# Two score matmuls per batch in place of three, with Q's halves stacked on the partitions

## The reference, cut to what matters

```python
x = x + einsum('bct,bcd->bdt', x, L0_weights[conditions])        # x is (32, 128, 1024)
q, k, v = (proj(x, W) for W in (Wq, Wk, Wv))                      # 16 heads of 64
q = q * minimum(cond, 4.0)                                        # one factor per batch
scores = einsum('bhqd,bhkd->bhqk', q, k) / sqrt(64)
scores = where(causal, scores, finfo.min)
attn = softmax(scores, axis=-1)
x = x + einsum('bsd,ed->bse', (attn @ v), Wo)
```

## Time and profile before

| | before |
|---|---|
| median of 3 runs | 1558.01 us (1557.51 to 1558.75) |
| the profiled execution | 1558.96 us |
| its span | 1557.5 us |
| TensorE busy | 1547.1 us, 99% |
| VectorE busy | 1034.9 us, 66% |
| ScalarE busy | 840.9 us, 54% |
| GpSimd busy | 866.6 us, 56% |
| granted TensorE clock, mean | 0.998 of 2.4 GHz |

### The profile page before, as it was taken

The page is one execution under the profiler, slowest core; times in us unless marked ns, Lnnn a source line. Parts: engine busy times, 40 slices in busy tenths (PEclk is TensorE's granted clock), DMA queues, the critical chain, the costliest instruction groups (busy, mean ns, idle before and its releaser), DMA issues.

```text
span 1557.5 us, 23477 instructions
## 1 busy us (share of the span) xinstructions
PE 1547.1 (99%) x7459; PEld 1302.0 (84%) x7459; DVE 1034.9 (66%) x1891; ACT 840.9 (54%) x2286; POOL 866.6 (56%) x752
## 2 busy tenths in 40 slices
PE   9999999999999999999999999999999989999999
PEld 7888888888888888888888888888888878888887
DVE  5867677664477777777767777777777644555553
ACT  6666566652466666666655666666666622222220
POOL 1555665662365566557655576575577545555552
PEclk9999999999999999999999999999999999999999
DMA  9968988866766677767677466677665696444442
GB/s 324 335 230 278 319 307 296 294 254 231 273 190 198 201 214 209 205 184 191 182 240 229 147 179 202 194 200 200 180 188 157 237 366 226 162 168 163 162 167 83
DMA packets 192300, 341.46 MB, mean 219 GB/s; under 512 B 23986, under 2 KB 116402, under 8 KB 185010
## 3 DMA queue, kind: packets, MB, share of 16 engines
q1 hardware_dynamic: 191026, 331.59, 66.2%
q10 hardware_dynamic: 1152, 8.39, 1.4%
HBM read 184.70 MB, written 134.22 MB: 205 GB/s over the span
## 4 chain that ended last, share of the span: by engine, by line
PE 95%; DVE 2%; DMA 1%; SPq 1%; POOL 0%; issue 0%; ACT 0%; DVEq 0%; POOLq 0%
PE p_PJ L768 22%; PE p_PJ L769 22%; PE p_PJ L770 22%; PE p_SC L770 6%; PE p_SC L769 6%; PE p_SC L768 6%; PE p_PV L873 4%; PE p_LP L768 1%; PE p_PV L768 1%; PE p_PV L770 1%; PE p_PV L769 1%; PE p_LP L770 1%; PE p_LP L769 1%; DVE t_WSL L1285 1%; DVE t_TS L1281 1%; DMA out<-t_xr 0%
## 5 line engine op out<-in xcount | busy, mean ns | idle before, releaser
L769 PE MATMUL p_PJ<-t_XL,t_WH 128*128 128x512 f32 x1008 | 394.2, 391 | 0.0
L768 PE MATMUL p_PJ<-t_XH,t_WH 128*128 128x512 f32 x1008 | 394.2, 391 | 0.0
L770 PE MATMUL p_PJ<-t_XH,t_WL 128*128 128x512 f32 x1008 | 392.1, 389 | 0.0
L1118 ACT ACTIVATE t_PP<-t_PP,t_st 128x128 f32<-128x128 f32 x512 | 199.5, 391 | 174.9 <-DVE t_st L1314 173.3
L1438 POOL TENSOR_TENSOR t_PP<-t_PP,t_st 128x512 f32<-128x512 f32 x128 | 133.2, 1041 | 205.8 <-DVE t_st L1318 205.8
L770 PEld LDWEIGHTS p_PJ<-t_XH,t_WL 128*128 128x128 f32 x1008 | 189.3, 188 | 40.5
L768 PEld LDWEIGHTS p_PJ<-t_XH,t_WH 128*128 128x128 f32 x1008 | 190.0, 188 | 33.8
L769 PEld LDWEIGHTS p_PJ<-t_XL,t_WH 128*128 128x128 f32 x1008 | 190.0, 188 | 32.3
L1332 DVE TENSOR_REDUCE t_AT<-p_PV 64x256 f32<-64x512 f32 x252 | 171.3, 680 | 24.5 <-ACT t_AC L1136 12.1
L1444 POOL TENSOR_TENSOR t_AT<-t_AT,t_AC 128x256 f32<-128x256 f32 x126 | 117.1, 929 | 126.2 <-DVE t_AT L1332 126.2
L1441 POOL TENSOR_TENSOR t_PS<-t_PT,t_PS 128x512 fp32r<-128x512 f32 x122 | 157.6, 1292 | 0.0
(11 more groups left out here) (259 smaller groups left out, 3597.7 us busy)
## 6 DMA issues: line engine op xcount, KB each, us to landing
t_XH<-xth_scratch SPq DMA_DIRECT2D x56, 512.0 KB, 6.4
t_XL<-xtl_scratch SPq DMA_DIRECT2D x56, 512.0 KB, 6.7
t_PT<-t_TB SPq DMA_DIRECT2D x580, 32.0 KB, 2.3
v_scratch<-t_VR SPq DMA_DIRECT2D x64, 256.0 KB, 4.6
xth_scratch<-t_XH SPq DMA_DIRECT2D x16, 1024.0 KB, 4.5
xtl_scratch<-t_XL SPq DMA_DIRECT2D x16, 1024.0 KB, 6.8
t_VX<-v_scratch SPq DMA_DIRECT2D x32, 512.0 KB, 5.6
at_scratch<-t_AT SPq DMA_DIRECT2D x126, 128.0 KB, 3.4
```

What stands on the lines that cost most here:

```text
L768: pe.matmul(bank, lh, rh, start=first, stop=False, skip_group_check=goes_on)
L769: pe.matmul(bank, lh, rl, start=False, stop=False, skip_group_check=goes_on)
L770: return pe.matmul(bank, ll, rh, start=False, stop=last, skip_group_check=goes_on)
L1118: act.activation(PP[:, u, h, :], PP[:, u, h, :], ACT.Exp, bias=st[:, 0, u, h:h + 1], scale=1.0, accum_out=st[:, 1, u, h:h + 1]).then_inc(a ...
```

## The change

The two operands are stacked in another way. For each head h there is one tile `QM[h]` whose 64 rows of that head hold Q's high part, and whose other 64 rows hold Q's low part of the same head. `KM[h]` has 256 columns for each batch: the first 128 hold K's high part in all 128 rows (twice, once for each half of the rows), the last 128 hold K's low part in the head's rows and zero in the others. One matmul of 256 columns for each head then gives high by high plus low by high in its first 128 columns, and high by low in its last 128. The two are added by VectorE: first the low product with the mask into `PP`, then the high product, in place, waiting on the first. The scores of the batches go round three banks (SC0, SC1 and LP), one for each batch, where two batches shared a bank.

The due times change with it: Q is evicted later, `a` is 7 steps after the end of the K block in place of 5, and scores, masks and exps are spread out. The K evictions stay at 0.25 and 1 step after the block. `QM` and `KM` stand for `QH`, `QL`, `KH`, `KL`, with the same sizes.

```diff
-                late = 2.5 if n else 0
+                late = 5 if n else 0
                 q_ev.put(done + late, n)
                 ql_ev.put(done + late + 1, n)
                 done += 8
                 kh_ev.put(done + 0.25, n)
                 kl_ev.put(done + 1, n)
-                a = done + 5
+                a = done + 7
                 for u in range(GB):
-                    k = u // 2
-                    sc_at.put(a + k, GB * n + u)
-                    mask_at.put(a + 1 + 2 * k, GB * n + u)
-                    exp_at.put(a + (2, 3, 4, 5)[u], GB * n + u)
-                move_at.put(a + 10, n)
+                    sc_at.put(a + (0, 0.5, 1, 3.5)[u], GB * n + u)
+                    mask_at.put(a + (1, 2, 3, 4.75)[u], GB * n + u)
+                    exp_at.put(a + (2.25, 3.25, 4.25, 6)[u], GB * n + u)
+                move_at.put(a + 10.25, n)
                 for k in range(2):
                     P = 2 * n + k
-                    recip_at.put(a + 4 + 2 * k, P)
-                    norm_at.put(a + 4.25 + 2 * k, P)
-                    turn_at.put(a + 7.5 + 1.5 * k, P)
+                    recip_at.put(a + (5, 7)[k], P)
+                    norm_at.put(a + (5.25, 7.25)[k], P)
+                    turn_at.put(a + (8, 9.75)[k], P)
                     last = n == 4 * NGRP - 1
-                    half_at.put(a + (20 if last else 25.25) + 0.5 * k, P)
-                    ptl_at.put(a + (20.75 if last else 26) + 1.5 * k, P)
-                    v = a + (27.25 + 3.25 * k if last else 29 + 4.5 * k)
+                    half_at.put(a + (22.5 if last else 25.25) + 0.5 * k, P)
+                    ptl_at.put(a + (23.25 if last else 26) + 1.5 * k, P)
+                    v = a + (29.25 + 3.25 * k if last else 29 + 4.5 * k)
                     own = v + (1.75 if n >= 4 * NGRP - 2 else (1.75, 8.5)[k])
...
-            early = t - PAIR
+            early = t - PAIR + (5 if q == 0 else 0)
...
+            if U == 2:
+                pe.wait_ge(dve_X, 2 * B)
+            if U >= 3:
+                pe.wait_ge(dve_s, U - 2)
+            for h in range(2):
+                mm = pe.matmul(s_bank(U)[:, h].rearrange("p l k -> p (l k)"), QM[h][:, cols], KM[h][:, u, :], start=True, stop=True)
+            mm.then_inc(pe_sc, 1)
...
-                        act.activation(KH[r, :, 128 * h:128 * h + 128], pj[r], ACT.Copy).then_inc(act_k, 1)
+                        other = slice(64 - 64 * h, 128 - 64 * h)
+                        act.activation(KM[h][r, :, 0:128], pj[r], ACT.Copy).then_inc(act_k, 1)
+                        act.activation(KM[h][other, :, 0:128], pj[r], ACT.Copy).then_inc(act_k, 1)
...
-                    act.activation(QH[:], PJ[bank_of["q", n]][:], ACT.Copy).then_inc(act_q, 1)
+                    for h in range(2):
+                        r = slice(64 * h, 64 * h + 64)
+                        act.activation(QM[h][r], PJ[bank_of["q", n]][r, :], ACT.Copy).then_inc(act_q, 1)
...
-                        dve.wait_ge(act_k, 2 * n + h + 1)
-                        dve.tensor_tensor(KL[r, :, k], pj[r], KH[r, :, k].bitcast(f32), ALU.subtract).then_inc(dve_k, 1)
+                        dve.wait_ge(act_k, 4 * n + 2 * h + 2)
+                        dve.tensor_tensor(KM[h][r, :, 128:256], pj[r], KM[h][r, :, 0:128].bitcast(f32), ALU.subtract).then_inc(dve_k, 1)
                 for n in ql_ev(tick):
-                    dve.wait_ge(act_q, n + 1)
-                    dve.tensor_tensor(QL[:], PJ[bank_of["q", n]][:], QH[:].bitcast(f32), ALU.subtract).then_inc(dve_q, 1)
+                    for h in range(2):
+                        r, other = slice(64 * h, 64 * h + 64), slice(64 - 64 * h, 128 - 64 * h)
+                        dve.wait_ge(act_q, 2 * n + h + 1)
+                        dve.tensor_tensor(QM[h][other], PJ[bank_of["q", n]][r, :], QM[h][r].bitcast(f32), ALU.subtract).then_inc(dve_q, 1)
...
+                    dve.scalar_tensor_tensor(out=PP[:, u], in0=s_bank(U)[:, :, 1], scalar=beta[:, bb:bb + 1],
+                                             in1=mask[:].unsqueeze(1).to_broadcast([128, 2, 128]), op0=ALU.mult, op1=ALU.add).then_inc(dve_l, 1)
+                    dve.wait_ge(dve_l, U + 1)
+                    dve.scalar_tensor_tensor(out=PP[:, u], in0=s_bank(U)[:, :, 0], scalar=beta[:, bb:bb + 1],
+                                             in1=PP[:, u], op0=ALU.mult, op1=ALU.add).then_inc(dve_s, 1)
```

More of the change, by code:

```diff
@@ L162, in cond_attention @@
             LATE = tile
[L163 to L166, removed]
+        KM = [sb(f"KM{h}", [128, GB, 256], f32r) for h in range(2)]
+        QM = [sb(f"QM{h}", [128, T], f32r) for h in range(2)]
         with nc.sbuf_tensor("t_PS", [128, 8, 2, 128], f32r) as tile:
@@ L205, in cond_attention @@
         act_Y, pool_Y = sem("y_high"), sem("y_low")
+        dve_l = sem("s_low_masked")
         dve_s, dve_m, act_e, dve_r = sem("masked"), sem("row_max"), sem("exp"), sem("row_recip")
@@ L654, in operand @@
             else:
-                halves = QH[:], QL[:]
+                halves = QM[0][:], QM[1][:]
             return tuple(four(h) for h in halves)
@@ L758, in pe_wait_bank @@
             if kind == "q":
-                pe.wait_ge(dve_q, i + 1)
+                pe.wait_ge(dve_q, 2 * i + 2)
             elif kind == "k":
@@ L848, in pe_v_step, with s_bank @@
                 mm.then_inc(pe_P, 1)
+        def s_bank(U):
+            return (SC[0], SC[1], LP)[U % 3][:].rearrange("p (h l k) -> p h l k", h=2, l=2)
         def pe_scores(U):
@@ L854, in pe_scores @@
                 pe.wait_ge(dve_k, 2 * n + 2)
+                pe.wait_ge(act_k, 4 * n + 4)
             if U == 0:
@@ L1181, in dve_turn @@
                 dve.wait_ge(s_O, 32 * 32)
+                dve.wait_ge(l_P, 160 * n)
             elif k == 0:
@@ L1301, in dve_program @@
                     bb = GROUP[n // NC] * GB + u
+                    dve.wait_ge(pe_sc, U + 1)
+                    if U == 0:
+                        dve.wait_ge(l_const, 32)
+                        dve.wait_ge(dve_beta, 1)
                     if n and u == 0:
                         dve.wait_ge(dve_t, 2 * n)
-                    dve.wait_ge(pe_sc, GB * n + 2 * (u // 2) + 2)
-                    if U == 0:
-                        dve.wait_ge(l_mask, 16)
-                        dve.wait_ge(dve_beta, 1)
-                    dve.scalar_tensor_tensor(
-                        out=PP[:, u], in0=SC[u // 2][:, 256 * (u % 2):256 * (u % 2) + 256].rearrange("p (h k) -> p h k", h=2), scalar=beta[:, bb:bb + 1],
-                        in1=mask[:].unsqueeze(1).to_broadcast([128, 2, 128]), op0=ALU.mult, op1=ALU.add).then_inc(dve_s, 1)
+                    dve.scalar_tensor_tensor(out=PP[:, u], in0=s_bank(U)[:, :, 1], scalar=beta[:, bb:bb + 1],
[3 more added lines that the diff above has]
+                                             in1=PP[:, u], op0=ALU.mult, op1=ALU.add).then_inc(dve_s, 1)
                 for U in mask_at(tick):
@@ L1404, in pool_program @@
                         pool.wait_ge(s_x1[z], 16 * x1_stores(z))
[L1405 to L1406 removed]
+                    pool.memset(KM[0][:].bitcast(f32), 0.0).then_inc(pool_z, 1)
+                    pool.memset(KM[1][:].bitcast(f32), 0.0).then_inc(pool_z, 1)
                 if tick == (T_ATT - 8) * TICK:
@@ L1730, in sp_program @@
                 if tick == 0:
-                    sp.dma_start(mask[:], mask_d).then_inc(l_mask, 16)
-                    sp.dma_start(beta[:], cond.to_broadcast([128, B])).then_inc(l_cond, 16)
+                    sp.dma_start(mask[:], mask_d).then_inc(l_const, 16)
+                    sp.dma_start(beta[:], cond.to_broadcast([128, B])).then_inc(l_const, 16)
                 for bb in l0_load(tick):
```

10 lines of the change are left out of this document (3 added, 7 removed).

## The result

| | before | after |
|---|---|---|
| median | 1558.38 us (4 runs, 1557.51 to 1559.41) | 1788.9 us (4 runs, 1785.96 to 1789.71) |
| ratio | | 1.148 (95% interval 1.146 to 1.150) |
| span of the profiled execution | 1557.5 us | 1786.9 us |
| mean granted clock | 0.998 | 0.941 |

The change costs 230 us. The forecast was 1664 and the range ended at 1710: the direction was right, the size was not. The page of the changed kernel: busy time of the engines, and the chain that ended last.

The account below looks back on a forecast made before the run. TensorE bounds the kernel before; afterwards VectorE's chain through own1 makes it wait. 48 x 1.80 + 13 x 1.60 = 107.2, less 1.4, gives +105.8: 1664 us against the median, range 1612 to 1710.

Parts of the forecast that it names:

- The two ties: Own1 queues behind K's low part on VectorE, half of P behind a K eviction on ScalarE; even PV awaits both.
- Who releases the PV: Own1, VectorE's reduction into AT, releases the even PV in 61 cells; TensorE idles 2.05 us a cell.
- the sum: Loop from even PV to next: 14.93 us against 13.33, +1.60 a cell, +1.80 in cells with a split.
- 1.3 us idle in the first 5 us left the clock at 1.00, and 2 us lies nearer to that: Argument against TensorE's clock falling when it idles 2.05 us in each attention cell.
- case B: TensorE's clock falls after the idle: 1817 us if in every cell, 1703 in a quarter; chance 0.12.
- a mild B: Clock falling in only some cells, which the range takes in; a quarter of the cells gives 1703 us.
- The price of the unknown operation: VectorE's second scale-and-add, four a cell: taken at 0.473 to 0.477 us; ends 0.41 (1649) and 0.69 (1717).
- The rule weighed: Skill page's rule that VectorE semaphores cost nothing extra: would save 0.9 us, loop 14.05; forecast kept 0.11 a hand-off.
- Rival A: VectorE hand-offs are cheap and the boundary after a K block paces the cell: 14.31 us, 1616 in all; chance 0.17.
- Rival C: TensorE stays the bound, own1 and half of P done within 12.88 us: faster, 1528 us; chance 0.03.
- bare VectorE work already 0.3 over: VectorE's work of 13.2 us a cell, without waits, exceeds the 12.86 TensorE would need.
- Rival D: No change: the saved 0.47 us a cell and the stall cancel; chance 0.02.

Follow-up runs that it names:

- the version of 1553.8: Changed kernel reordered (masks in pairs, splits earlier), then second half of P later and GpSimd's norm and low half ahead of its A^T product: 1553.8 us, ratio 0.997.
- the run with nine filler matmuls: Changed kernel plus nine unread 512-column matmuls on TensorE ahead of each even PV's wait: 1700.7 us, clock 0.998.

## Why the prediction was wrong, and where it was right

- **The two ties**: right. Each is enough for a slow loop (1673.2 in the kernel before with own1's alone, 1721.2 with the half of P's alone), and undoing both takes 174 us off.
- **Who releases the PV**: right. Own1, 62 times; idle 2.15 us where 2.05 was forecast, and 2.58 with a split where the sum has 2.25. The half of P comes under it, by 0.6 to 0.7 us and not by the forecast's 0.5 and 0.2: at full clock its chain gives cells of 14.56 and 15.10, own1's 15.27 and 15.67.
- **The step that failed: "1.3 us idle in the first 5 us left the clock at 1.00, and 2 us lies nearer to that".** The clock fell in all cells of the loop but one, which is case B, given 0.12. The cost was 88 us. B was over-priced for every cell (153) and under-weighted as a case; the range reached only "a mild B". This is why 1789 lay outside it. Full clock would have given about 1701, inside.
- **Its evidence was misread too.** The clock column of the earlier trace rows says 1.00, but the nine matmuls of that stretch took 647 ns on average:

```profile
L948 PE MATMUL p_PJ<-t_PRH 128*128 128x512 f32 x9 | 4.2, 647 | 1.3 <-POOL t_PRH L1397 1.3
```

The same shape takes 0.63 us at 1.2 GHz (905.31 in the rows of after) and 0.39 at 2.4 GHz, so TensorE ran that stretch slowly whatever the column says. The 1.3 us also lie ahead of its first matmul, so they cannot show what an idle does to an engine at work. What was left was one idle of 3.95 us that lost the clock, and no row for 2 us. When a clock column matters, read the distance of the matmuls beside it.

- **Terms of the sum that were too small.** At full clock a plain cell took 15.27 for 14.93, one with a split 15.67 for 15.13: 48 x 0.54 + 13 x 0.34 = 30 us. In both, the masks and maxima of four batches took 5.48 for 5.40, second transpose to K's low part 0.73 to 0.75 for 0.61, own1 to PV 0.14 for 0.03. A split added 0.40 where 0.20 was forecast, and in another place: the sum made K's low part wait for ScalarE, but it follows the second transpose at once (1045.85, 1046.58), and what is longer is VectorE's subtraction ahead of that, 1.13, for which the sum had no term. With the 30 us the forecast at full clock would have been 1694. The 7 us up to 1701 are not accounted for.
- **The price of the unknown operation**: right, 484 ns for 477.
- **The rule weighed**: a hand-off measures 0.52 between starts against 0.39 to 0.40 between free neighbours (two in 0.87). So the statement of the Trainium skill, page "VectorE: DVE Perf Modes", section "The DRAIN you can't avoid", that a semaphore between costs nothing extra, which the page measured on eight tensor_copy, does not hold for these operations. With the batches in pairs, where no operation waits for the one just ahead, VectorE's busy time fell by 41.7 us.
- **Rival A**: that both ties undone give 1615.0 and rival A had 1616 is chance. A kept the ties and let the boundary pace the cell; the run has no ties, and VectorE's round paces it. **Rival C**: its 12.86 came true in the cells without a split once the order was remade, and "I see only a misreading of the two ties that would give it" holds for the change as made. But "bare VectorE work already 0.3 over" does not hold for these cells: its 13.2 took VectorE's share from a stretch in which every cell has a split, and with the pairs VectorE is busy for 11.5 us of such a cell (46.00 of 51.36 over four, in the version of 1553.8). **Rival D** did not happen.

What stays open: 7 us of the sum, and why four cells take 14.65 us, three of them eight cells apart. In their ScalarE rows a copy for Wo waits 2.7 us for a store, which points at a buffer, but no run tested it. What decides, besides its length, whether an idle loses the clock is open too.

## What to carry to other kernels

When a change shifts due times, look in each engine's program for work that another engine needs soon and that now shares a tick with something queued ahead of it: here the two ties were worth 86 us at full clock, and own1's alone 115 in the kernel before. If a forecast lets TensorE idle once a cell, and the trace has no idle of that length, price the half clock behind it as a case of its own with a real chance. A form of the work that is cheaper on the bounding engine (0.47 us a cell here) can pay, but only when the order is made for it, and when the engine that takes the load has room: with VectorE busy for 90% of a plain cell and 94% of one with a split, 4 us of the 30 were left here (46.00 of 51.36 us over four plain cells and 37.32 of 39.50 over three with a split, in the version of 1553.8).

## What was not expected of the hardware

- TensorE's clock after an idle ahead of a PV: behind 0.7 to 1.86 us the matmuls stayed at 2.4 GHz, behind 1.91 to 2.60 us they ran at 1.2 GHz for a while (904.51 to 907.87 in the rows of after), and the cell took 1.4 to 1.6 us longer. One idle of 2.16 us, in the run with nine filler matmuls, is the exception: the clock stayed (1376.69).
- A subtraction of two SBUF tiles (128x512) on VectorE took 0.69 us with GpSimd starting behind it, and 1.13 to 1.26 beside GpSimd's work. GpSimd's product for A^T went from 0.74 to 1.24 in turn.
- Copies of 64 rows to the other half of the partitions cost ScalarE nothing extra: 0.59 and 0.59.
